# A 32-pair vision tower with L1 attention on one core: new slot tables, and the last layer norm moved to ScalarE

## What is computed

```python
# token part: three convolutions with a layer norm ahead of each, a last norm, a projection
h = relu(conv2d(layernorm(x), conv1)); h = relu(conv2d(layernorm(h), conv2)); h = relu(conv2d(layernorm(h), conv3))
h = layernorm(concat of the halves of h) @ out_w + out_b            # (64, 128, 64)
# attention part, on x = layernorm(h): 8 heads, scores are L1 distances
v = x @ wqv + b; q, vf, vb = v in thirds; k = x[:, :, None, :] * wk
a = softmax(-sum_w |q[s, h, w] - k[t, h, w]| / sqrt(64) over s, with a zero row added)
o = (a applied to vf + a transposed applied to vb), summed over heads
h = h + x + (o * sigmoid(1.702 * o)) @ fanin + b
# expert part: argmax router over 32 experts, relu MLP 64 -> 16 -> 64
h = h + relu(relu(x @ W1[idx] + b1[idx]) @ W2[idx] + b2[idx])       # x = layernorm(h)
```

## Time and profile before

| | us |
|---|---|
| median of 3 timed runs | 3565.9 |
| lowest and highest of them | 3556.08, 3571.57 |
| the profiled execution, its own time | 3552.77 |
| its span from first to last instruction | 3551.0 |
| mean granted clock of TensorE | 0.987 |

### The profile page before, as it was taken

The page is one execution under the profiler, slowest core; times in us unless marked ns, Lnnn a source line. Parts: engine busy times, 40 slices in busy tenths (PEclk is TensorE's granted clock), DMA queues, the critical chain, the costliest instruction groups (busy, mean ns, idle before and its releaser), DMA issues. The chain is left out here.

```text
span 3551.0 us, 78815 instructions
## 1 busy us (share of the span) xinstructions
PE 3291.4 (93%) x23174; PEld 2433.9 (69%) x23174; DVE 3124.4 (88%) x4452; ACT 2691.1 (76%) x4796; POOL 2845.6 (80%) x2728
## 2 busy tenths in 40 slices
PE   8899999999999999999999999999999999999888
PEld 6676666766666776666776667766677666676655
DVE  6888989988999889988899988889898898888886
ACT  3777877777787777777777877777777777777774
POOL 3878888888888888887888888888888888888874
PEclk9999999999999999999999999999999999999999
DMA  6778778778787788777787877777777877777874
GB/s 140 157 152 161 152 152 159 153 153 162 154 159 151 154 158 159 156 150 144 154 164 152 162 147 155 157 156 155 155 153 154 163 151 157 151 154 152 164 156 86
DMA packets 198693, 543.75 MB, mean 153 GB/s; under 512 B 68054, under 2 KB 132438, under 8 KB 145656
## 3 DMA queue, kind: packets, MB, share of 16 engines
q0 software_dynamic: 73728, 501.78, 71.5%
q1 hardware_dynamic: 124920, 41.40, 6.1%
HBM read 10.79 MB, written 2.10 MB: 4 GB/s over the span
## 5 line engine op out<-in xcount | busy, mean ns | idle before, releaser
L918 DVE TENSOR_REDUCE S<-psU 128x16 f32<-128x1024 f32 x2182 | 2612.0, 1218 | 284.3 <-PE psU L481 276.1
L481 PE MATMUL psU<-flat,kT 99*128 99x256 bf16 x16384 | 2325.4, 276 | 223.0 <-ACT absd L706 104.4
L706 ACT ACTIVATE absd<-psU 128x1024 f32<-128x1024 f32 x1914 | 1953.0, 1024 | 626.8 <-PE psU L481 602.4
L481 PEld LDWEIGHTS psU<-flat,kT 99*128 99x128 bf16 x16384 | 1494.0, 98 | 911.3 <-DVE S L918 241.2
L1193 POOL TENSOR_TENSOR absd<-absd 128x1024 f32<-128x1024 f32 (+2 forms) x512 | 1173.6, 2292 | 204.3 <-DMA absd<-absd 203.1
L1182 POOL DMA_DIRECT2D absd<-absd x512 | 453.8, 886 | 296.3 <-ACT absd L706 250.2
L1197 POOL TENSOR_TENSOR absd<-absd 128x512 f32<-128x512 f32 (+2 forms) x512 | 609.5, 1190 | 40.2
L1200 POOL TENSOR_TENSOR absd<-absd 128x256 f32<-128x256 f32 (+2 forms) x512 | 351.5, 687 | 40.2
L493 PE MATMUL psC<-c1in,w 128*128 128x384 f32 (+1 forms) x930 | 312.1, 418 | 1.5 <-DVE c1in L962 0.8
L585 PE MATMUL psZ<-P,v 128*128 128x256 f32 x1024 | 309.0, 384 | 0.3 <-ACT P L824 0.3
L512 PE MATMUL psC<-c3in,w 128*128 128x128 f32 x1240 | 255.6, 290 | 5.2 <-DVE c3in L962 5.1
(11 more groups left out here) (178 smaller groups left out, 2212.7 us busy)
## 6 DMA issues: line engine op xcount, KB each, us to landing
absd<-absd POOLq DMA_DIRECT2D x413, 1024.0 KB, 7.9
flat<-qparts SPq DMA_DIRECT2D x3072, 8.0 KB, 4.0
absd<-absd POOLq DMA_DIRECT2D x64, 768.0 KB, 6.7
absd<-absd POOLq DMA_DIRECT2D x35, 512.0 KB, 4.8
xin<-in_x SPq DMA_DIRECT2D x32, 192.0 KB, 7.9
flat<-pattern SPq DMA_DIRECT2D x4, 768.0 KB, 10.7
out_h<-result SPq DMA_DIRECT2D x32, 64.0 KB, 5.9
w<-in_w SPq DMA_DIRECT2D x1, 1280.0 KB
```

The lines of the kernel that those rows point to most:

```text
L481: mm = nc.tensor.matmul(psU[:, slot % PLACES, m], kT[0:ROWS + 3, b, m, :], flat[0:ROWS + 3, half % HALVES, :, lo:lo + BLOCK], start=True, ...
L706: nc.scalar.activation(absd[:, c % GROUPS, :, u], psU[:, slot % PLACES].rearrange("p (n a) s w -> p n (a s w)", n=2), ACT.Abs).then_inc(a_ ...
L918: nc.vector.tensor_reduce(S[:, b, hd, SB * c:SB * c + SB], psU[:, slot % PLACES].rearrange("p a s w -> p s a w"), AX.XY, ALU.add, apply_ab ...
```

## The change

1. `AT_AT` and `KQ_AT` become tables per batch entry (`AT0`, `AT1`, `KQ0`, `KQ1`), and nearly every number in these and in the other tables is new.
2. `SHARED` changes in two chunks: chunk 2 shares heads (1, 2, 3, 4) and not (0, 2, 4, 6); chunk 14 shares (2, 4, 6) and not (0, 3, 6). `LAST_AFTER` goes from 17 to 21. `SHARED_LAST` is new from chunk 8 on.
3. The last token norm runs on ScalarE, as scale * y + shift with shift = -mean * rstd. GpSimd makes the shift behind the root, with two more instructions.
4. Ahead of `qparts` ScalarE waits once for `made` (units done) where it waited for four load semaphores; in the lead-in three waits of ScalarE for weight loads go. The built ScalarE loop has 264 instructions after and 265 before, waits and register work included.

```diff
-SHARED = [(0, 2, 4, 6), (0, 2, 4, 6), (0, 2, 4, 6), (0, 2, 4, 6), (1, 3, 5), (0, 2, 4, 6), (0, 2, 4, 6), (0, 2, 4, 6),
-          (0, 2, 4, 6), (0, 2, 4, 6), (0, 2, 4, 6), (3, 6), (0, 2, 4, 6), (0, 2, 4, 6), (0, 3, 6), (0, 2, 4, 6)]
+SHARED = [(0, 2, 4, 6), (0, 2, 4, 6), (1, 2, 3, 4), (0, 2, 4, 6), (1, 3, 5), (0, 2, 4, 6), (0, 2, 4, 6), (0, 2, 4, 6),
+          (0, 2, 4, 6), (0, 2, 4, 6), (0, 2, 4, 6), (3, 6), (0, 2, 4, 6), (0, 2, 4, 6), (2, 4, 6), (0, 2, 4, 6)]
...
-LAST_AFTER = 17
+LAST_AFTER = 21
...
-SHARED_LAST = {12: (1, 5), 13: (2, 4, 6), 14: (1, 5), 15: (0, 2)}
+SHARED_LAST = {8: (0, 2, 4, 6), 9: (2, 6), 10: (0, 2, 4), 11: (0, 4), 12: (1, 3, 5), 13: (0, 2, 4, 6), 14: (1, 5), 15: (0, 3)}
...
-KQ_AT = dict(kT=21, q=13, q_len=1, qpart1=13, qrest1=14, qpart2=38, qpart3=37)
-AT_AT = dict(vf=0, vb=7, v_len=0, turn_len=0, exp=20, exp_len=8, rden=27, scale=30, scale_len=8, turna=42, turnb=45,
-             pv=47, pv_len=8, half=52, sum=53, tanh=54, gate=58)
+KQ0 = dict(kT=22, q=13, q_len=0, qpart1=12, qrest1=13, qpart2=29, qpart3=37)
+KQ1 = dict(kT=15, q=11, q_len=1, qpart1=11, qrest1=13, qpart2=35, qpart3=32)
+KQ_AT = (KQ0, KQ1)
+AT0 = dict(vf=1, vb=7, v_len=0, turn_len=1, exp=20, exp_len=11, rden=32, scale=34, scale_len=7, turna=42, turnb=45,
+           pv=47, pv_len=7, half=52, sum=53, tanh=54, gate=55)
+AT1 = dict(vf=3, vb=6, v_len=0, turn_len=0, exp=20, exp_len=5, rden=27, scale=29, scale_len=13, turna=42, turnb=45,
+           pv=47, pv_len=5, half=52, sum=53, tanh=55, gate=56)
+AT_AT = (AT0, AT1)
...
-HAND_AT = dict(xT=12, hx=65)
-TOK_AT = dict(copy=0, a=10, conv1=21, len1=22, b=45, conv2=55, len2=10, c=65, conv3=75, len3=32, d=108, turn=122,
-              out=126, root=0, gap=7)
...
+HAND_AT = dict(xT=6, hx=89)
+TOK_AT = dict(copy=0, a=10, conv1=21, len1=22, b=44, conv2=55, len2=10, c=65, conv3=75, len3=30, d=108, turn=122,
+              out=125, root=0, gap=6)
...
-WARM = 44
...
+WARM = 36
...
-STILL = dict(turna=50, fan=16, turn=31, route=9, turnoh=14, hida=2)
+STILL = dict(turna=35, fan=7, turn=33, route=0, turnoh=13, hida=8)
...
+                if slot == TOK_AT["d"] + TOK_AT["gap"]:
+                    act.wait_ge(by_pool, TOK_POOL.after(q, "shiftd"))
...
+                    for b in range(2):
+                        nc.scalar.activation(resn[:, b, :], z[:, b * 2 * J:(b + 1) * 2 * J], ACT.Identity,
+                                             bias=nmr["d"][:, b:b + 1], scale=rstd["d"][:, b:b + 1]).then_inc(by_act, 1)
...
-                        for n in range(HALVES):
-                            act.wait_ge(flat_in[n], 48 * (4 * CHUNKS // HALVES * (p - 1) + 2 * CHUNKS // HALVES * (b + 1)))
+                        act.wait_ge(made, SLOTS * (p - 1) + 64 * (b + 1))
...
-                if slot == TOK_AT["d"] + TOK_AT["gap"]:
-                    dve.wait_ge(by_pool, TOK_POOL.after(q, "rstdd"))
-                    lead("turn")
-                    for b in range(2):
-                        nc.vector.tensor_scalar(resn[:, b, :], rows(2 * J)[:, b, :], mv["d"][:, b, 0:1],
-                                                rstd["d"][:, b:b + 1], ALU.subtract, ALU.mult).then_inc(by_dve, 1)
...
+                        if name == "d":
+                            shift("d", by_pool, lambda s: TOK_POOL.after(q, s + "d"))
```

86 lines of the change are left out of this document (43 added, 43 removed).

## The result

| | before | after |
|---|---|---|
| median of 13 runs, us | 3559.5 (3553.1 to 3571.6) | 3549.4 (3538.5 to 3555.4) |
| ratio, 95% interval | | 0.9965 (0.9954 to 0.9977) |
| profiled execution, span | 3551.0 | 3547.6 |
| pairs 1 to 30 together | 3246.3 | 3241.9 |
| median pair, of 3 to 29 | 107.6 | 107.6 |

The ratio and its interval come from the comparison of the timed runs and are not the quotient of the two medians. The change is worth 10 us, a third of one per cent, where 49 had been forecast. An ordinary pair is not shorter. The kernel before came out 6 us lower over 13 runs (3559.5) than over the three from which the forecast was counted (3565.9), so the measured 3549.4 lies only 32 us above the forecast of 3517, although the change itself missed by 39. The profiled executions differ by 3.4 us, of which pair 30 gives 3.3; the medians differ by 10.

A forecast was written before the change was run, and what follows sets the result against it. The bound was taken to change by stretch among TensorE, VectorE and ScalarE. -1.2 us a pair gives -36 over 30 pairs; disturbed pairs -12 and tail make -49, from 3565.9 to 3517 us; range 3465 to 3565.

The forecast's parts named there:

- Slots 0 to 11: Value copy and x1T_late ahead of the norm fill ScalarE's wait for nmrn; VectorE gates: -0.3 us a pair.
- Slots 11 to 22: Chunk 2's new shared heads leave VectorE one D slot fewer before slot 22: -0.6 us a pair, bounds -1.13 and +0.5.
- Slots 22 to 64 and 83 to 96: TensorE gates; its instructions are the same in number and kind, only shifted: 0, bounds +-0.3 us.
- Slots 64 to 83: VectorE's wait for the tree goes, ScalarE's wait for the same sum is late next: 0 us taken, 0 to -0.2.
- Slots 96 to 109: ScalarE gates and its eight scale instructions come later and denser: +0.3 us a pair, bounds 0 and +0.6.
- Slots 109 to 128: The norm leaves VectorE, taking off 0.72 us: -0.6 us a pair taken, bounds 0 and -0.9.
- GpSimd breaks even on its two products: Slots 109 to 128: two products cost 0.5 us with gaps, but GpSimd's 0.65 us wait for qparts goes.
- The last sums: Slots 64 to 83: LAST_AFTER = 21 gives GpSimd four more slots; 0 to -0.2 us, gain mainly in disturbed pairs.
- Disturbed pairs: About 19 us lost in a few pairs; -12 us, from fewer late trees and a shorter TensorE pause before slot 11.
- Lead-in 0, tail -1: Lead-in: key parts earlier, second norm later, 0, bounds -2 and +1.5 us. Tail: 15 idle matmuls fewer, -1 us.
- the second: Rival: TensorE gates after all, VectorE's savings become idle; 3554 to 3566 us, taken as 3560; chance 0.16.
- the third: Rival: TensorE's clock halves in most pairs, at slots 17 to 24; 3594 us if in all 30; chance 0.10.

The follow-up runs named there:

- a_pv8: Changed kernel with the attention product of batch entry 1 spread over 8 slots instead of five: 3539.2 us, ratio 0.9949 to the kernel before.
- b_early: Kernel before with entry 1's value copies at slots 3 and 6 and the copy x1T_late at slot 6: 3549.0 us, ratio 0.9978.
- a_rootc_scale: Changed kernel with GpSimd's root of norm c ahead of the tree and entry 0's exponentials, reciprocal and scale at their old slots: 3550.0 us, ratio 0.9966.
- a_norm_dve: Changed kernel with the last token norm back on VectorE and GpSimd's two products gone: 3543.7 us, ratio 0.9954 to the kernel before.
- b_shift: Kernel before with only GpSimd's two products for norm d added, results unused, norm left on VectorE: 3592.7 us, ratio 1.0093.
- a_rootc: Changed kernel with only GpSimd's root of norm c moved ahead of the adding tree: 3522.3 us, ratio 0.9885 to the kernel before.
- a_fourwaits: Changed kernel with four load waits in place of the one on units, ScalarE's loop at 268 instructions: 3777.6 us, ratio 1.0608 to the kernel before.
- b_norm_act: Kernel before with the last token norm moved to ScalarE, old tables and four load waits kept: 3689.4 us, ratio 1.0376.
- b_norm_one: Kernel before with the last token norm on ScalarE and one wait on units in place of four: 3581.1 us, ratio 1.0058.

## Why the prediction was wrong, step by step

The forecast was -49 us: -36 in ordinary pairs, -12 in disturbed ones, -1 in the tail. The result is -10. Of the signs that I had named, most came: VectorE at 95.7 us in pair 10 (96.1 named for the mean pair), slots 0 to 22 at 17.2 (17.4), 96 to 109 at 9.6 (9.6), 109 to 128 at 14.9 (14.8), the wait for the tree near zero. Only the pair did not: 107.6 for 106.4. Of the 1.2 us between forecast and result 0.69 are in slots 22 to 59, 0.16 in slots 59 to 78 and the rest in four small pieces of 0.04 to 0.13.

Two steps failed. The first is the 0 for slots 22 to 64, where 0.69 us were lost. The second is the one that decides: in slots 64 to 83 I let VectorE's wait for the tree go and named ScalarE's wait for the same sum as what is late next. It is VectorE's own wait for `rstdc`, which GpSimd makes behind that tree. As long as the root stands there, slot 76 comes some 63.4 us after the pair's start, and a gain ahead of it does not get past: a_pv8 won 0.3 us of the first loss back, was 0.29 us ahead of before at slot 75 and 0.03 at slot 78. With the root moved 0.8 us a pair came out at the end.

- **Slots 0 to 11, -0.3 forecast:** -0.49 measured; b_early shows -0.46 with the early value copy and hand-over alone. Right in cause, a little small. The wait for `nmrn` is all but gone from ordinary pairs: of its 16.1 us in 14 waits 4.9 are in the lead-in and 9.1 in five pairs, and TensorE's pause before slot 11 is 0.55 us, below the 0.8 that I had named.
- **Slots 11 to 22, -0.6:** -0.28 against before, but undoing chunk 2 costs 0.61. The mechanism and its size are right; 0.3 us of other edits stand against it. The copy `qparts` now waits 58.9 us for TensorE in place of 29.0, 0.74 us at slot 12 of most pairs; that this is the 0.3 us is not shown. With the first stretch -0.9 was forecast at slot 22 and -0.77 came.
- **Slots 22 to 64 and 83 to 96, 0 +- 0.3:** +0.69 between slots 22 and 59. The first step that failed: "the same in number and kind, only shifted by a slot or two" overlooked that five slots for eight attention matmuls make three slots too long for the two engines behind them: 0.3 us (a_pv8). The other 0.4 is not attributed; 0.1 of it is there by slot 47.
- **Slots 64 to 83, 0:** +0.16 by slot 78 in the median pair. The step that decided the sum. I read who waits in the kernel before, and there VectorE's `c3in` waits for nobody in an ordinary pair, since it arrives at 61.6 us when `rstdc` is done at 61.5. A link that comes just in time leaves no row among the waits. The chain as a whole did leave one: of the 30.1 us for the tree 11.2 are at slots 73 to 75, in 14 pairs, and that tree ends 60.5 us after the pair's start, 1 us ahead of `rstdc`. I counted this wait as one that later last sums take away, and they did; the next link of the same chain stood 1 us behind. GpSimd's busy share of 80% said nothing of this chain of DMA landing, tree, arithmetic of norm e, tree, root of norm c. With the root moved by one slot a pair gains 0.74 us at slot 76, and the whole 27 us.
- **Slots 96 to 109, +0.3:** +0.36 measured, but a_rootc_scale shows that the cause named for it is wrong.
- **Slots 109 to 128, -0.6 from the norm:** -0.47 measured, and a_norm_dve has it without the norm's move. A right number for a wrong reason: VectorE's 0.72 us were not what the stretch ended on. What brings the 0.47 us was not looked for.
- **GpSimd breaks even on its two products:** true in the new table, as far as a_norm_dve shows, which takes norm and products out together and moves a pair by 0.1 us; in the old one they cost 1.8 us a pair (b_shift). I had put no price on them where that cover is missing.
- **The single wait, 0:** right for what it does to the waits, and the loop's length was looked at. But I took 264 or 265 for harmless without asking how far the edge is. With the norm on ScalarE as well, four waits in place of one cost 228 us.
- **The last sums, 0 to -0.2 and the disturbed pairs:** the wait for the tree went as forecast (30.1 to 4.0 us). Without it the new table loses 3 us a pair.
- **Disturbed pairs, -12 us:** pairs more than 1 us above the median had 21.9 us too much before and have 19.9 after. There are two kinds. Four pairs before lost the clock at slots 76 to 88 (3, 13, 14 and 26, at 0.77 to 0.88, the four of the loop's pairs with the longest waits for the tree there, 0.95 to 1.53 us), none do after; this is the kind for which the forecast was right. Pair 14 at that place before:

```profile
1634.75:1649.56 14.81, 14.00 (x82) 11.22 (x83) 9.76 (x14) 9.22 (x16) 9.47 (x8) 0.77 0.69 137
```

  GpSimd's late `nmrn` still makes the other kind, in pairs 1, 2, 14 and 21, and they are dearer than before. Pair 2 of the changed kernel: ScalarE's wait, TensorE's pause, and the stretch behind it:

```profile
284.07 0.77 ACT L760 ACTIVATE x<-h,nmrn,rstdn 128x64 f32<-128x64 f32 x2 [1.26 <-POOL nmrn L1222]
```

```profile
285.80 0.65 PE L486 MATMUL psU<-flat,kT 99*128 99x256 bf16 x4 [1.67 <-ACT absd L711]
```

```profile
286.50:297.00 10.50, 10.30 (x49) 7.09 (x49) 7.28 (x11) 6.13 (x9) 8.81 (x8) 0.52 0.76 151
```

  I had taken the 1.34 us pause of pair 10 for the cause (1.04 is the median pair's), and it did shrink. The pairs of the changed kernel that lose the clock at slots 11 to 22 are the four in which `nmrn` is late and the pause is 1.67 to 3.71 us; with 1.22 us pair 11 keeps it. The length alone does not decide: before, pair 19 lost the clock behind 1.29 us and pair 14 kept it behind 2.23.
- **Lead-in 0, tail -1:** the first unit starts 0.6 us later (56.65 us for 56.01), pair 0 is 0.5 shorter, and the last pair and tail are 0.8 us longer. The 1 us of the tail did not come, and no run asks why.

Of the rivals the second came nearest, in its time (3560) and in its sign of more VectorE idle at a pair of 107.5. Its reason, that TensorE gates, is not what a_rootc shows: TensorE's work in a pair is the same there, and the pair is 0.8 us shorter. The granted clock of the whole is 0.987 in both, so the third did not come.

## What to carry to other kernels

An engine that arrives just as its input does shows no wait, and a wait that a change takes away may stand only a little ahead of the next one of the same chain. So before pricing a change, list for each stretch what every waiting instruction would wait for next, with its time from the stretch's start; where that time is the same in several versions, it is the first candidate for the bound, whatever the busy shares say, and moving one piece of its chain tests it. Tables that hold each other's instructions apart are priced one edit at a time only by undoing one at a time: the later last sums are worth nothing in the old table and 3 us a pair in the new, and GpSimd's two products cost nothing in the new and 1.8 us in the old. The instructions of an engine's loop are counted when something is added to it (264 and 265 ran free here, 268 did not), and so are the packets of the fetching queues in every profile.

## What the runs showed of the hardware

- A ScalarE loop of 268 instructions in place of 264 or 265 brought 140 packets of instruction fetch and a stop of 3.6 to 4.7 us at each turn (median 3.9 in a_fourwaits, 3.8 in b_norm_act), on an engine that is busy 73 to 74% of the span.
- TensorE's granted clock at slots 11 to 22: before, with a median pause of 1.04 us ahead of slot 11, it stayed at 2.4 GHz in 27 of 30 pairs; with 1.43 to 1.45 us it was at 1.2 GHz for part of the stretch in 21 (b_shift) and 18 (b_norm_one) of 30. In b_shift pairs with the same pause, 1.42 to 1.44 us, did both. Repeated matmuls of 0.45 us ahead of the pause left 2 of 30. The Trainium skill ("TensorE: Matmul & The Clock Gate", Part 1) ties the level to how busy TensorE was of late, and the trace agrees.
- 0.55 us of work on GpSimd, which is idle 19 us of a mean pair, cost 1.8 us a pair: `nmrn` comes 0.4 us later, and the clock behind TensorE's longer pause falls more often.
